# Moving three groups of SBUF tiles by 64 or 32 bytes, and one ring of PSUM banks for the routed experts

## What is computed

```python
x = x + attention(conditioned(x, cond_8))       # L0: one head pair, causal
x = x + moe(expert_mlp(x))                       # L0: silu MLP, then 8 routed experts, top 2
x = x + gru(token_mlp(x))                        # L1: gelu MLPs, then a gated scan
x = x + ffn(adapted(x))                          # L1: LoRA product, then a ternary FFN

# routed experts of L0 (640 slots each): h = gelu(e @ W1a) * (e @ W1b);  y = h @ W2
# token MLP of L1, for three weight sets per sequence (two picked experts and the shared one):
out += w_e * (gelu(x @ gate) * (x @ up)) @ down  # 256 -> 1024 -> 256
# last FFN: gelu(x @ T1.T + b1) @ T2.T + b2      # 256 -> 1024 -> 256, weights -1, 0, 1
```

## Time and profile before

| | us |
|---|---|
| median of 3 runs | 939.68 (939.64 to 940.03) |
| profiled execution, device time | 939.6 |
| its span in the profile | 938.3 |
| PE busy with matmuls, of the span | 924.2 (98%) |
| PE busy with weight loads | 776.6 (83%) |
| DVE, ACT, POOL busy | 529.7, 446.8, 269.6 |

### The profile page before, as it was taken

One profiled execution on the slowest core, in us unless ns is written; L12 is line 12 of the kernel. 1 busy time (PEld: TensorE's weight loads), 2 busy tenths in 40 slices (PEclk: granted clock), 3 DMA queues, 4 the chain that ended last, 5 costly groups with the idle time before them and its releaser, 6 DMA issues.

```text
span 938.3 us, 13194 instructions
## 1 busy us (share of the span) xinstructions
PE 924.2 (98%) x4895; PEld 776.6 (83%) x4895; DVE 529.7 (56%) x972; ACT 446.8 (48%) x831; POOL 269.6 (29%) x243
## 2 busy tenths in 40 slices
PE   8999999999999999999999999999999999999998
PEld 4768868888799999998888888888888888888786
DVE  6754453586756766686565564334333335788544
ACT  3666565433355455574344344353343342345775
POOL 1533221220265765653420153042140230010000
PEclk9999999999999999999999999999999999999999
DMA  8030001202355444432513003003003002000011
GB/s 297 29 113 23 24 0 68 79 23 96 66 143 144 145 134 148 130 101 79 180 34 135 23 23 136 0 1 135 1 1 135 0 27 109 1 1 1 0 45 46
DMA packets 22193, 67.49 MB, mean 72 GB/s; under 512 B 4514, under 2 KB 11954, under 8 KB 19314
## 3 DMA queue, kind: packets, MB, share of 16 engines
q1 hardware_dynamic: 16546, 40.15, 11.8%
q0 software_dynamic: 5440, 26.50, 9.6%
q10 hardware_dynamic: 144, 0.00, 0.0%
HBM read 55.09 MB, written 9.45 MB: 69 GB/s over the span
## 4 chain that ended last, share of the span: by engine, by line
PE 87%; DVE 5%; issue 2%; ACT 2%; DMA 2%; POOL 0%; SPq 0%; ACTq 0%; DVEq 0%; POOLq 0%
PE banks L1087 18%; PE banks L1089 18%; PE banks L1088 18%; PE banks L1320 5%; PE banks L1322 5%; PE banks L1321 5%; PE banks L1179 3%; PE banks L1163 2%; PE banks L1372 2%; PE banks L1371 2%; PE banks L1170 2%; PE banks L1359 1%; PE banks L1358 1%; PE banks L1133 1%; DMA weight_stage<-in_cond_w 1%
## 5 line engine op out<-in xcount | busy, mean ns | idle before, releaser
L1087 PE MATMUL banks<-input_hi,mlp_hi 128*128 128x512 f32 x376 | 147.7, 393 | 0.0
L1089 PE MATMUL banks<-input_hi,mlp_lo 128*128 128x512 f32 x376 | 146.5, 390 | 0.0
L1088 PE MATMUL banks<-input_lo,mlp_hi 128*128 128x512 f32 x376 | 146.3, 389 | 0.0
L1582 ACT CAST hidden_hi<-hidden 128x512 fp32r<-128x512 f32 x96 | 59.6, 621 | 161.5 <-DVE hidden L1987 110.3
L2177 POOL TENSOR_TENSOR mlp_lo<-weight_stage,mlp_hi 128x768 fp32r<-128x768 f32 x32 | 58.9, 1841 | 172.6 <-ACT mlp_hi L1556 172.6
L1993 DVE TENSOR_TENSOR hidden_lo<-hidden,hidden_hi 128x512 fp32r<-128x512 f32 x96 | 66.4, 692 | 62.0 <-ACT hidden_hi L1582 61.7
L1987 DVE SCALAR_TENSOR_TENSOR hidden<-banks,L_expert_weight,gelu 128x512 f32<-128x512 f32 x64 | 48.1, 751 | 84.9 <-PE banks L1089 81.8
L1576 ACT ACTIVATE gelu<-banks 128x512 f32<-128x512 f32 x96 | 57.3, 597 | 63.7 <-PE banks L1089 63.6
L1089 PEld LDWEIGHTS banks<-input_hi,mlp_lo 128*128 128x128 f32 x376 | 70.6, 188 | 14.8
L1088 PEld LDWEIGHTS banks<-input_lo,mlp_hi 128*128 128x128 f32 x376 | 70.6, 188 | 14.4
L1087 PEld LDWEIGHTS banks<-input_hi,mlp_hi 128*128 128x128 f32 x376 | 70.6, 188 | 14.3
(11 more groups left out here) (333 smaller groups left out, 2174.7 us busy)
## 6 DMA issues: line engine op xcount, KB each, us to landing
weight_stage<-in_packF SPq DMA_DIRECT2D x8, 1536.0 KB, 8.1
weight_stage<-in_shared SPq DMA_DIRECT2D x2, 3072.0 KB, 10.3
expert_output<-y_rows SPq DMA_DIRECT2D x40, 128.0 KB, 2.1
weight_stage<-in_cond_w SPq DMA_DIRECT2D x4, 512.0 KB, 5.6
residual<-in_xT SPq DMA_DIRECT2D x4, 512.0 KB, 11.2
first_half_swapped<-first_half SPq DMA_DIRECT2D x16, 128.0 KB, 2.1
routed_input<-x_rows SPq DMA_DIRECT2D x16, 128.0 KB, 1.7
weight_stage<-in_ffn_w SPq DMA_DIRECT2D x2, 1024.0 KB, 8.3
```

The source lines that it names most:

```text
L1087: pe.matmul(o, wh, dh, start=(i == 0), stop=False)
L1088: pe.matmul(o, wh, dl, start=False, stop=False)
L1089: last = pe.matmul(o, wl, dh, start=False, stop=(i == len(terms) - 1))
L1582: act.copy(hiD[n % 4][:, :], prod_t[n % 2][:, :]).then_inc(done)
```

## The change

It does three things.

1. `down3` goes, and `w2` takes its banks from `work`, which is now the plain ring 0, 1, 2, 3, 6, 7 for `w1` and `w2` together.
2. A helper `behind(base, n)` moves `top[0]` up to the next address that lies n bytes past the place of `base` within a line of 256 bytes. It is called before `gathered`, before the hidden tiles of the token MLP (`hiD`, `loD`), both with 64, and before the hidden tiles of the last FFN (`hiE`, `loE`), with 32.
3. Nothing else: the orders of all engines are the same, instruction by instruction; 88 of the 819 units on PE get another bank.

After it, `dn` has its moving operand at 32 and its weights at 224, which is +64; `f2` has 0 and 224, which is +32; the transposes `xe` and `yt` have 32 and 32, which is 0. `gu`, `f1`, `w1` and `w2` keep 0. All tiles placed behind `gathered` in that phase (`y_rows`, `gelu`, `hidden`) begin 64 bytes later too; only DVE, ACT and DMA use them.

```diff
-    use("work", [(n,) for n in (0, 1, 2, 3, 6, 7) * 2 + (0, 1, 2, 3)])
+    use("work", [(n,) for n in (0, 1, 2, 3, 6, 7)])
     use("turn3", [(4,), (5,)])
-    use("down3", [(6,), (7,)])
...
     def down_expert(e):
         for j in range(ST):
-            product("down3", "w2", e, j)
+            product("work", "w2", e, j)
...
+    LINE = 256
+
+    def behind(base, n):
+        top[0] += (base + n - top[0]) % LINE
...
+    behind(phase_top, 64)
     got_at = top[0]
     got = [sb("gathered", [P, D]) for _ in range(ST + 1)]
...
     wDl.append(sb("mlp_lo", [P, PK1], F32R))
+    behind(phase_top, 64)
     hiD = [sb("hidden_hi", [P, CH], F32R) for _ in range(4)]
     loD = [sb("hidden_lo", [P, CH], F32R) for _ in range(4)]
...
+    behind(phase_top, 32)
     hiE = [sb("hidden_hi", [P, CH], F32R) for _ in range(4)]
     loE = [sb("hidden_lo", [P, CH], F32R) for _ in range(4)]
```

## The result

The change makes the kernel slower: 946.22 us in the median of five runs (945.76 to 947.16) against 940.03 for the kernel before, run beside it; ratio 1.0073, 95% interval 1.0061 to 1.0084. The forecast was 936.4 us and its range ended at 945.0; both are missed, and the side is the wrong one. The profiled execution was the longest of the five: 947.16 us, with a span of 945.9 us in the profile.

What follows compares the result with a forecast made beforehand. PE's matmul start distances bound the kernel; -0.9 us (ring) and -2.4 us (`dn`), all else 0, sum to -3.3 us: 936.4 us. The range for 8 times in 10 was 932 to 945 us.

Steps and rivals of the forecast that it cites:

- What bounds the kernel: Whole kernel: PE is busy 98% at full clock, so moved tiles pay only through the distance between matmul starts.
- Part 1: Expert stage, one ring of banks: PE's waits for `yrow` copies go, 0.9 us gained (ends: nothing and 1.0).
- Part 2: Token MLP, `dn` at +64: 576 matmuls gain 4.2 ns each, 2.4 us (ends: 3.6 gained, 3.7 lost).
- Part 4: Token MLP, `gu` between moved `dn`: changes of place taken to cost 0; otherwise up to 4.9 us, `f1` 0.6.
- Part 3: Last FFN, `f2` at +32: 128 matmuls, between 0.8 us lost and 0.8 us gained, taken as 0.
- Part 5: `gathered` and tiles behind it: 112 transposes with both operands at one place, at most 0.7 us either way, taken as 0.
- The step is lost: Rival, chance 0.30: MLP and last FFN matmuls slow down, 948.8 us, or 943.3 if `gu` keeps its step.
- The place does not matter: Rival, chance 0.20: addresses change no distance between matmuls, only the ring of banks pays, 938.8 us.
- worst third: Whole-kernel range: the part of the slower rival's outcomes that the prediction said its range, up to 945, left out.

Runs made afterwards that it cites:

- a1_ring: The kernel before with only the new ring of banks (`w2` takes its banks from `work`), all tiles where they were; ratio 0.9982.
- a3_ffn32: The kernel before with only the hidden tiles of the last FFN at +32; last FFN 65.42 us, device time 1.4 us more.
- u64: The kernel before with `input`, `gathered` and all L1 hidden tiles 64 bytes past the weights' place, old banks; token MLP 399.35 us.
- a4_gath64: The kernel before with only `gathered` and the tiles behind it at +64, so the transposes have both operands at one place; ratio 0.9997.
- a2_mlp64: The kernel before with only the token MLP's hidden tiles at +64 (`gathered` 256 bytes further for room); token MLP 402.46 us, device time 6.1 us more.
- u32: The kernel before with `input`, `gathered` and all L1 hidden tiles 32 bytes past the weights' place, old banks; 233.3 ns per 512 columns.
- b224: The kernel before with the new ring, second-sequence L0 MLP weights and output weights moved from -32 to 0; 937.25 us, ratio 0.9981.
- s64: The kernel before with every tile 64 bytes further, so all differences between operands stay the same; its time is not given in the text.
- m64: The kernel before with the inputs at +64 and the hidden tiles at 0, old banks; `dn` takes 231.6 ns.

## Why the prediction was wrong, by its own steps

- **What bounds the kernel** was right: PE's clock and what bounds it did not change, and the whole loss came through the distance between starts.
- **Part 1**, the ring: right in sign and cause, too small, because the earlier trace rows were misread. Both waits went, and nothing took their place. `a1_ring` shortens the stage by 1.57 us where I had 0.9 and a bound of 1.0. "Both are the fifth `w2` of an expert waiting for the third's copy" holds for one of the two waits, that of 0.50 us at 413.20. The other is the third `w2` of expert 3 (counted from 0, as experts 6 and 7 are), which waited for the first's copy:

```profile
341.92 0.39 PE L1087 MATMUL banks<-ffn_w_hi,expert_hidden_hi 128*128 128x256 f32 x1 [0.24 <-DVE y_rows L1926]
```

The stop at 434.59 is the fourth `w2` of expert 7, behind the second's copy (it ends at 434.5), and too short to be among the waits; so is one more at 411.00, the fourth of expert 6, behind a copy that ends at 410.9. Distance by distance against `a1_ring`, the two stops that were priced gave back 1.00 us, the sum's own bound, and the two that were left out 0.31 and 0.14 us. The last 0.12 us stand in a wait for `gathered`, a DMA, at 259 us, and `a3_ffn32`, without the ring, is 0.10 us shorter there too.

- **Part 2** failed: "I take the -64 rows and their mean, 4.2 ns: 576 x 4.2 = 2.4 us gained". The rows were of 256 columns. I carried them to 512 because the remainder of 13.3 ns was the same for both widths, but that had been seen only at 0. Off 0 the two widths part: -64 is 113 to 118 ns against 120.0 at 256 columns, and 233.3 against 226.7 at 512. `dn` loses 231.7 - 226.8 = 4.9 ns, 2.8 us; 2.2 ns of that are the price of +64 itself (`u64`), the rest comes with the steps. The row of the right width, 6.4 ns more at -32, had the sign and was within 1.5 ns.
- **Part 4** failed: "I take 0 here, as the forecast's condition". `gu` rises from 227.2 to 230.5 ns, 1128 x 3.3 = 3.7 us; my bound was 4.9. With Part 2 that makes 6.5 us, where 6.4 were measured in the token MLP. It was the largest term, put at nothing without a reason, and a row already showed that such a disturbance takes ten matmuls to die away, in a unit of twelve.
- **Part 3** failed in size: "I take 0, as the sign is open". `f2` rises to 232.1 and `f1` to 231.5 ns, 128 x 5.4 + 128 x 4.8 ns = 1.3 us.
- **Part 5** was right: `a4_gath64`, 0.9997.
- **The rivals.** "The step is lost" was the mechanism, between its two prices (943.3 and 948.8 us). Its tipping point, `gu` above 229.6 ns, was crossed with 230.5. "The place does not matter" falls with `a2_mlp64`, `a3_ffn32` and `u32`. With it falls, for this kernel, what was drawn from the rule that spoke for it: the Trainium skill, "TensorE: Matmul & The Clock Gate", "Step-by-step: what each phase is for", has the weight load take no read bandwidth from the running matmul, so that no address should change the distance. The traces disagree with that: with nothing changed but addresses, the same 512 columns take 226.7 to 233.3 ns. Whether read bandwidth is what is lost they do not show.
- **The range** ended at 945.0, less than a third of the way between the two prices of a rival to which I gave 3 in 10 (943.3 and 948.8); it left out more than the "worst third" that the prediction names. With the term of -64 rows struck out, the same rows would have given a loss.

## What to carry to other kernels

Take the price of an address from rows of the same width and the same kind of product; a gain at 256 columns was a loss at 512 here. Where one side of two neighbouring products is moved, price the neighbour as well, above all if it runs for fewer matmuls than a disturbance needs to die away. And before moving tiles at all, write down the differences modulo 256 of every pair: groups that lie apart by accident (here two at -32) are the cheap gains, 0.6 us in `b224`. In this kernel that meant 0 for products of 512 columns and -64 for those of 256.

## What was not expected of the hardware

- 512 columns of fp32r take 226.7, 233.3, 228.9, 232.4 and 233.3 ns at a difference of 0, 32, 64, 128 and 192 bytes; 256 columns take 120.0 at 0, 117.6 at +64, some 118 at -32, and 113.3 to 118 at -64. That the remainder above one column per cycle of 2.4 GHz depends on the width was the surprise. What in PE's reads makes it is not shown by these runs; I only know that the difference counts and not the address (`s64`). Since all weights of a stage lie at one place, the runs don't tell either whether a matmul's own weights or those of the next one count.
- A matmul's distance depends on those up to ten before it (kernel after, `gu` 1 to 12). In `m64`, six products at the best place never settle at their 226.7 ns between others at +64.
- Chips differ by 5 us for the same kernel (944.57 and 944.88 us against 939.34 to 940.03 for the kernel before), most of it through one stall in the expert stage. Each of the chips on record was used in one session, so it may be the session too. In the profile of `u64` the granted clock is 0.52 for 3.3 us behind it.
